# Reordering TensorE's instructions in the attention loop of an adaLN + mixture-of-experts layer

## The reference

```python
ada = (timestep_embed @ ada_w + ada_b)[:, None, :]
shift1, scale1, gate1, shift2, scale2, gate2 = jnp.split(ada, 6, axis=-1)
x1 = _ln(x) * (1.0 + scale1) + shift1
qkv = (x1 @ qkv_w + qkv_b).reshape(Bc, Tc, 3, H, DH)
q, k, v = (qkv[:, :, 0], qkv[:, :, 1], qkv[:, :, 2])
attn = jnp.einsum('bthd,bshd->bhts', q, k) * DH ** (-0.5)
attn = jax.nn.softmax(attn, axis=-1)
attn_out = jnp.einsum('bhts,bshd->bthd', attn, v).reshape(Bc, Tc, INNER)
x = x + gate1 * (attn_out @ out_w + out_b)
x2 = _ln(x) * (1.0 + scale2) + shift2
x = x + gate2 * (gelu(x2 @ ffn_w1 + ffn_b1) @ ffn_w2 + ffn_b2)
# then: top-4 of 16 experts (176 wide) for each token, a shared expert (704 wide), and the residual
```

## Time and profile before

| | busy us | share of the span |
|---|---|---|
| TensorE, matmuls (PE) | 908.5 | 92% |
| VectorE (DVE) | 616.8 | 62% |
| ScalarE (ACT) | 481.8 | 49% |
| GpSimd (POOL) | 307.1 | 31% |

### The profile page before, as it was taken

One profiled execution on the slowest core, in us unless ns is written; L12 is line 12 of the kernel. 1 busy time (PEld: TensorE's weight loads), 2 busy tenths in 40 slices (PEclk: granted clock), 3 DMA queues, 4 the chain that ended last, 5 costly groups with the idle time before them and its releaser, 6 DMA issues.

```text
span 991.4 us, 17761 instructions
## 1 busy us (share of the span) xinstructions
PE 908.5 (92%) x5692; PEld 812.3 (82%) x5692; DVE 616.8 (62%) x1447; ACT 481.8 (49%) x1296; POOL 307.1 (31%) x231
## 2 busy tenths in 40 slices
PE   4899999999999999989999999999959899999950
PEld 4788988989899898979898778788848789999940
DVE  5864446454464544664465777666785777777748
ACT  2545454454554545534545555654513545555520
POOL 1330303012020120270001615666751654444430
PEclk9999999999999999999999999999979999999985
DMA  5999961010010100120002004245302433334338
GB/s 187 342 353 352 339 211 49 0 48 0 0 48 0 48 0 0 48 86 22 1 23 98 23 22 140 79 159 198 102 11 65 159 109 118 119 112 123 115 125 314
DMA packets 73043, 107.77 MB, mean 109 GB/s; under 512 B 6793, under 2 KB 61198, under 8 KB 72720
## 3 DMA queue, kind: packets, MB, share of 16 engines
q1 hardware_dynamic: 31280, 53.10, 16.4%
q10 hardware_dynamic: 34832, 36.77, 11.8%
q0 software_dynamic: 6864, 17.06, 4.6%
HBM read 50.99 MB, written 57.87 MB: 110 GB/s over the span
## 4 chain that ended last, share of the span: by engine, by line
PE 80%; DVE 14%; issue 2%; POOL 2%; DMA 1%; ACT 1%; SPq 0%; POOLq 0%; DVEq 0%; ACTq 0%
PE bank L1335 45%; PE bank L1707 8%; PE bank L1419 6%; PE bank L1398 5%; PE bank L1730 5%; PE bank L1407 3%; PE bank L1667 3%; DVE acc L1324 3%; PE bank L1693 2%; PE bank L1718 2%; DVE hid_area L846 2%; DVE work L1221 1%; DVE work L1299 1%; POOL hs L537 1%; DVE work L915 1%
## 5 line engine op out<-in xcount | busy, mean ns | idle before, releaser
L1335 PE MATMUL bank<-tok_area,arena_a 128*128 128x512 f32 x768 | 208.4, 408 | 4.9 <-DVE tok_area L846 4.4
L846 DVE TENSOR_TENSOR hid_area<-bank,hid_area 128x256 fp32r<-128x256 f32 (+2 forms) x222 | 110.8, 499 | 114.9 <-ACT hid_area L627 107.2
L1335 PEld LDWEIGHTS bank<-tok_area,arena_a 128*128 128x128 f32 x768 | 139.4, 192 | 30.4 <-DVE tok_area L846 4.8
L612 ACT ACTIVATE work<-bank,negm 128x128 f32<-128x128 f32 x256 | 90.5, 367 | 92.3 <-DVE negm L908 92.2
L605 ACT ACTIVATE work<-bank,bqk_sb 128x512 f32<-128x512 f32 x128 | 88.2, 689 | 74.9 <-PE bank L1335 74.9
L1335 PE MATMUL bank<-arena_a,tok_area 128*128 128x256 f32 x768 | 108.6, 291 | 0.0
L371 POOL TENSOR_TENSOR arena_a<-raw,fixed 128x1536 fp32r<-128x1536 f32 x7 | 19.2, 2747 | 274.8 <-DMA bv_sb<-in_bv 274.8
L549 POOL DMA_INDIRECT ys<-work,dest x79 | 76.9, 973 | 86.4 <-DVE dest L1303 80.5
L1707 PE MATMUL bank<-wE,hid_area 128*128 x474 | 98.3, 343 | 5.1 <-DVE hid_area L846 5.1
L1335 PEld LDWEIGHTS bank<-arena_a,tok_area 128*128 128x128 f32 x768 | 97.0, 193 | 0.0
L1335 PE MATMUL bank<-hid_area,x_area 128*128 128x512 f32 x384 | 96.1, 399 | 0.0
(11 more groups left out here) (160 smaller groups left out, 1596.5 us busy)
## 6 DMA issues: line engine op xcount, KB each, us to landing
hs<-h_even ACTq DMA_DIRECT2D x1, 35904.0 KB, 119.1
work<-hs SPq DMA_DIRECT2D x79, 132.0 KB
we_raw<-in_we SPq DMA_DIRECT2D x16, 608.0 KB, 5.6
y_all<-ys SPq DMA_DIRECT2D x8, 1024.0 KB, 12.1
raw<-in_wqkv SPq DMA_DIRECT2D x8, 768.0 KB, 4.4
work<-in_x SPq DMA_DIRECT2D x4, 512.0 KB, 6.3
raw<-in_wo SPq DMA_DIRECT2D x8, 256.0 KB, 4.3
raw<-in_w SPq DMA_DIRECT2D x2, 1024.0 KB, 5.9
```

The costliest lines, as they stand in the source:

```text
L612: last = nc.scalar.activation(probs[:, m, i], SC_BANK[m][:, i * T:i * T + T], ACT.Exp, bias=negm[:, m, i:i + 1], scale=SCALE, accum_out=rs ...
L846: return nc.vector.tensor_tensor(target, whole, high.bitcast(f32), ALU.subtract)
L1335: last = nc.tensor.matmul(out_ap, stationary(s), moving(m), start=start and i == 0, stop=stop and i == len(PARTS) - 1)
```

## The change

In TensorE's stream T1 moves ahead of P3, directly behind V0; V1 moves behind P5; S1 moves ahead of P0. The order becomes S0, S1, P0, O, P1, T0, P2, V0, T1, P3, P4, P5, V1. VectorE's order follows in one place: L1 moves behind A1, so it runs n1, L0, A0, A1, L1. The two steps with extra work keep their own VectorE order (step 29: L0, statistics, A0, normalisation, L1, A1; step 30: L0, A0, L1, `low2`, A1). ScalarE's, GpSimd's and the load queue's programs are the same. In step 29 the transposes that `late` issues now stand behind T1.

```diff
@@ VectorE, tail @@
                 normal(it, j, base, 1)
-                for m in range(2):
-                    low_o(it, j, m)
-                    if more:
+                low_o(it, j, 0)
+                if more:
+                    for m in range(2):
                         project_v(it, j + 1, m)
+                low_o(it, j, 1)
@@ TensorE @@
             def first_half(it, j, more):
                 scores(it, j, 0)
+                scores(it, j, 1)
                 if more:
                     project(it, j + 1, 0)
-                scores(it, j, 1)
...
                 values(it, j, 0)
+                turn_probs(it, j, 1)
                 if late:
                     late(0)
                 if more:
-                    project(it, j + 1, 3)
-                turn_probs(it, j, 1)
-                if more:
-                    project(it, j + 1, 4)
+                    for tile in range(3, 6):
+                        project(it, j + 1, tile)
                 values(it, j, 1)
-                if more:
-                    project(it, j + 1, 5)
```

## The result

The changed kernel takes 999.16 us, the median of nine runs, against 993.25 us before. The ratio is 1.0061, with a 95% interval of 1.0046 to 1.0075: slower by 0.6%. Forecast were 998.1 us and a range of 993.0 to 1001.0. (The comparison leaves disturbed runs out; one of the nine took 3199.8 us.)

A forecast was written before the change was run, and what follows sets the result against it. The prediction took TensorE's own stream to bound the steady loop. Its terms, -1.8 + 0 + 4.7 + 0.5 + 1.5 = +4.9 us on 993.2, gave 998.1 us, with a range of 993.0 to 1001.0.

The forecast's parts named there:

- the joints: Switches between fp32 and fp32r runs on TensorE: fewer of them, 0.02 us net each, -1.8 us over 30 steps.
- step 25: VectorE's negation 0, 0.41 us later, is held by GpSimd's split of w1, so T0 starts late: +4.7 us.
- step 1: Negation 0 comes later and may be held by GpSimd's first piece: even chance of 1.1 us, carried as +0.5.
- The clock in step 25: Half-clock stretch behind TensorE's longer idle at T0: expected the same as before, no more.
- rival D: Longer idles bring one more stretch at half clock, 1.7 us of work lost, 999.8 us; chance 15%.
- Steps 30 and 31: L1 waits for late V1 in step 30, delaying n0 and T0 of step 31: +1.5 us.
- rival C: A joint between fp32 and fp32r runs costs 0.10 us, not 0.02, so the kernel is faster, 990.9 us; chance 8%.
- T1 early: T1 directly behind V0 waits for n1 in no steady step, since GpSimd's split comes earlier too: cost 0.
- V1 late: V1 behind P5: P4's and P5's banks are copied in time; L1 behind A1 makes negation 0 0.41 us later.
- the 997.2 us run: One of three runs of the kernel before, read as one where GpSimd's piece in step 25 came earlier.

The follow-up runs named there:

- experiment 4: Changed kernel with one extra GpSimd instruction (256 columns, about 0.55 us) ahead of w1's split in step 24: 996.24 us, ratio 1.0027.
- experiment 5: Kernel before with one extra GpSimd instruction (about 0.6 us) ahead of w1's split: 994.09 us, ratio 1.0009.
- experiment 7: Changed kernel with w1's and w2's splits in four parts each: 989.04 us, ratio 0.9962.
- experiment 8: Kernel before with w1's and w2's splits in four parts each: 987.48 us, ratio 0.9948.
- experiment 6: Changed kernel with VectorE's order in step 30 as L0, A0, low2, A1, L1: 997.48 us, ratio 1.0047.
- Experiment 1: Kernel before with S1 alone moved, directly behind S0 and ahead of P0: 992.39 us, ratio 0.9988.
- experiment 9: Changed kernel with w1's and w2's splits in four parts, pair 1's projection weights in three, and step 30's low2 early: 984.57 us, ratio 0.9915.
- experiment 11: Kernel before with V1 behind P5 and L1 behind A1, plus ScalarE's copy of P3 ahead of its copy of T1: 999.53 us, ratio 1.0067.
- experiment 3: Kernel before with V1 and L1 alone moved, behind P5 and behind A1: 1004.95 us, ratio 1.0104.
- experiment 2: Kernel before with T1 alone moved, directly behind V0: 994.39 us, ratio 1.0012.

## Why the prediction was right

Forecast were +4.9 us and the two profiles differ by 6.3. The mechanism and the largest term are right. That the sum is off by only 1.4 is partly luck: the joints came 1.6 us worse than forecast and step 25 0.5 worse, while step 1 (0.1 where 0.5 stood) and the part behind the attention (-0.3, not forecast) gave 0.7 back.

**The sum came out by its largest term.** Step 25 was forecast at +4.7 and measured at +5.2. The chain of waits inside it came as written: negation 0 at 433.42 (forecast 433.54) and held to the piece's end, negation 1 to the second piece's, n0 behind the third, T0 at 446.55 (forecast 446.67), n1 free. Experiments 4, 5, 7 and 8 show that the piece, its place and its length are the cause: moved 0.6 us it gives 3 us back to the changed order and none to the old one, and cut in four it gives 10 and 5 us back. The rule of the Trainium skill that I weighed ("SBUF — State Buffer", Who interferes with whom) holds here in numbers: tensor_scalar 4.42 in place of 0.17 us, tensor_tensor with two SBUF inputs 4.98 in place of 0.69, tensor_reduce from PSUM 0.68 beside a running piece.

**The clock in step 25** was taken as unchanged and wasn't quite: P2 and V0 behind T0 take 4.29 us (451.61 - 447.32) at a granted 0.50, where P2 and V0 took 445.96 - 442.41, 3.55, and P3 was slow in part. With T0 it is 1.10 us more for T0, P2 and V0 and 0.3 less for P3. By the balance, 5.24 less the 4.55 by which T0 is later leaves 0.7 us for it. That is under half of rival D, whose full +1.7 didn't come.

**Steps 30 and 31**: forecast +1.5, measured +1.4, and experiment 6 takes it back.

**Joints: the term that failed.** Forecast -1.8 us, measured -0.2. I had worked the net price of a joint from S0 and S1 in front of P0, 0.02 us, and put it on all three joints that go. A joint costs the run behind it a lead-in and gives the run before it 0.08 back; for a 128x512 run the lead-in is 0.10, for a 128x256 run it is 0.08, so it is free. Two of the three stood before P4 and P5, of 128x256. Experiment 1, which removes the one before a 128x512 run, has a step 0.013 us shorter; the changed kernel 0.007, where 0.06 was forecast. The 0.10 a joint of rival C was never near.

**Step 1** was carried at an even chance of 1.1. Both numbers were off. Of the seven profiles with V1 late, six have negation 0 passing, by 0.04 to 0.12 us (the changed kernel by 0.10, experiments 4, 6, 7, 9 and 11 by 0.09, 0.12, 0.05, 0.12 and 0.04); it is held in experiment 3 alone, by 0.02, where P5's wait has made it 0.1 us later. So in the changed kernel it mostly passes, by a margin that one could not have forecast. And the price was too low: held, it cost 2.2 us (2.3 less the 0.1 of P5's wait), since the longer idle (2.66 us) also brought low clock, which I had put into the bound only.

**T1 early** was forecast at 0 and is 0, for the reason given (GpSimd's pieces come 0.8 to 1.3 us earlier, 0.8 forecast); experiment 2, which leaves the loads where they were, has the small waits.

**V1 late.** I wrote that P5's bank would be read in time. That is so in the changed kernel and only there: with T1 in its old place ScalarE copies P3 too late, at 0.1 us a step and 2.2 us more in step 1 (experiments 3 and 11). The early T1 is what makes the late V1 cheap; I had not seen that the two depend on each other.

**The median before.** I took the 997.2 us run for one in which negation 0 was held. Experiment 1's profile shows such an execution in nearly the old order, 4.2 us above its median (996.62 against 992.39); that the 997.2 run was one is still only argued.

## What to carry to other kernels

On a saturated TensorE an order is worth what it does to the engines beside it. Before moving something, list the small instructions behind it on each engine with their distance to the next long instruction of the engine that can hold them, and give every distance that is not well above your shift (0.41 us here) a price in whole instructions. Then cut the long instruction: four pieces of 128x512 in place of one of 128x2048 were worth 5 us in the old order and 10 in the new, more than any order of TensorE's stream here. Where two moves are made together, ask of each what it costs alone; one may be paying for the other.

## What the runs showed of the hardware

A 128x4 tensor_scalar of 0.17 us was held for up to 4.6 us by one GpSimd tensor_tensor. It got in when that ended (437.84, the next piece having started at 437.78), and the next VectorE instruction within SBUF, started at 438.47, was held by that next piece. Starting 0.01 us ahead of a piece or 0.01 us behind it made the whole difference (experiments 2 and 1). GpSimd's 128x2048 instruction of line 371 took 3.60 us with nothing held behind it (429.53) and with negation 1 held for 2.93 us (437.78). That of line 373 took 4.50 to 4.62 us where VectorE was held, and 4.9 where n0 was still running at its start (441.47, n0 to 441.94): the one that comes second pays.

TensorE, idle for 7.85 us, had a granted 0.50 from 447.0 to 451.5; after 3.2 us idle it had 0.57 over 443 to 447. After a wait of 3.89 us in experiment 5 it worked slowly until about 449 us (P2 2.70, V0 1.56, P3 1.78). From T0's start to V0's end it took 2.72 us in experiment 7, where T0 of step 25 doesn't wait, but 3.95 (experiment 3), 4.24 (6), 4.52 (1), 5.04 (11) and 5.06 us (the changed kernel) behind waits of 7.6 to 7.9 us. So behind nearly the same idle the slow stretch costs over 1 us more in one execution than in another. How much of this kernel's scatter that makes is not shown.
